# Masked cross-attention layer rewritten: strip scores, unnormalised weights, new queue order

## What is computed

```python
q = split_heads(layernorm(x) @ Wq + bq); k = split_heads(ctx @ Wk + bk); v = split_heads(ctx @ Wv + bv)
scores = einsum('bhqd,bhkd->bhqk', q, k) / sqrt(16)
scores = where(mask[:, None, :, :] > 0, -1e9, scores)
p = softmax(scores, axis=-1)
x = x + merge_heads(einsum('bhqk,bhkd->bhqd', p, v)) @ Wo + bo
```

## Time and profile before

| | us |
|---|---|
| median of 3 runs | 3196.28 (3191.54 to 3201.59) |
| the profiled execution | 3201.86 |
| its span, first to last instruction | 3200.1 |
| start of the program, weights, statistics | 0 to 34 |
| masked cross-attention | 34 to 1047 |
| state space layer | 1047 to 1586 |
| quantised network | 1586 to 1740 |
| sigmoid cross-attention (the other attention layer) | 1740 to 2436 |
| self-attention | 2436 to 2775 |
| experts | 2775 to 3200 |

### The profile page before, as it was taken

One profiled execution on the slowest core, in us unless ns is written; L12 is line 12 of the kernel. 1 busy time (PEld: TensorE's weight loads), 2 busy tenths in 40 slices (PEclk: granted clock), 3 DMA queues, 4 the chain that ended last, 5 costly groups with the idle time before them and its releaser, 6 DMA issues. The chain is left out here.

```text
span 3200.1 us, 85879 instructions
## 1 busy us (share of the span) xinstructions
PE 2706.9 (85%) x32700; PEld 2118.3 (66%) x32700; DVE 2312.3 (72%) x5209; ACT 1905.3 (60%) x4534; POOL 1931.9 (60%) x2135
## 2 busy tenths in 40 slices
PE   3999999999998489998677999999995788546998
PEld 2877777777777355555344788888884666434776
DVE  4999999999998387777634677777775788663443
ACT  2666767676666577767233677777773666343333
POOL 4888788888885477777300766666662677233332
PEclk9999999999999688988688999999997999757999
DMA  5121111111110000000000221111210000352110
GB/s 144 42 61 61 42 61 50 53 61 42 61 48 2 20 1 1 1 1 1 14 16 16 93 61 57 53 59 61 61 47 16 2 2 2 121 182 74 38 38 28
DMA packets 87375, 143.57 MB, mean 45 GB/s; under 512 B 10784, under 2 KB 74144, under 8 KB 80704
## 3 DMA queue, kind: packets, MB, share of 16 engines
q1 hardware_dynamic: 82304, 123.52, 12.4%
q0 software_dynamic: 4672, 14.57, 1.3%
HBM read 123.37 MB, written 14.69 MB: 43 GB/s over the span
## 5 line engine op out<-in xcount | busy, mean ns | idle before, releaser
L376 POOL TENSOR_SCALAR x_prob<-x_prob,x_rs 128x257 f32<-128x257 f32 x512 | 247.8, 484 | 173.1 <-DVE x_rs L852 141.6
L705 ACT ACTIVATE x_prob<-x_prob,x_nm 128x257 f32<-128x257 f32 x512 | 254.3, 498 | 152.6 <-DVE x_nm L846 152.5
L2119 DVE TENSOR_TENSOR_SCAN m_s<-m_a,m_psD 128x1024 f32<-128x1024 f32 x128 | 284.9, 2267 | 2.3 <-PE m_psD L1946 2.2
L1420 DVE SCALAR_TENSOR_TENSOR x_pTl<-x_psS,x_pTh 128x1024 f16<-128x1024 f32 x128 | 156.7, 1225 | 145.3 <-ACT x_pTh L1328 145.3
L843 DVE CUSTOM_DVE_ANT_0 x_prob<-x_psS,x_masked,x_prob 128x256 f32<-128x256 f32 x512 | 217.3, 481 | 4.5
L2058 ACT ACTIVATE m_a<-m_dt,m_rate 128x248 f32<-128x248 f32 x512 | 206.8, 492 | 0.0
L1108 POOL TENSOR_TENSOR x_qbdh<-x_qh,all_mask4h 128x1024 f16<-128x1024 f16 x32 | 60.6, 1895 | 217.5 <-DVE x_ql L1401 217.5
L1830 POOL TENSOR_TENSOR m_s<-m_s 128x1024 f32<-128x1024 f32 x64 | 150.5, 2352 | 67.8 <-DVE m_s L2119 67.8
L3003 ACT ACTIVATE e1t_g<-e1t_psH,e1t_bias 128x128 f32<-128x128 f32 x312 | 89.2, 368 | 171.0 <-PE e1t_psH L2952 171.0
L689 ACT ACTIVATE x_kh<-x_psK,x_bk 128x256 f16<-128x256 f32 x256 | 107.5, 471 | 118.6 <-PE x_psK L263 116.1
L861 DVE TENSOR_TENSOR x_pTl<-x_psT,x_pTh 128x512 f16<-128x512 f32 x256 | 164.2, 682 | 5.6 <-ACT x_pTh L676 3.0
(11 more groups left out here) (599 smaller groups left out, 11913.9 us busy)
## 6 DMA issues: line engine op xcount, KB each, us to landing
x_ctx<-in_ctxT SPq DMA_DIRECT2D x32, 1028.0 KB, 6.3
x_ctx<-in_ctxT SPq DMA_DIRECT2D x32, 1024.0 KB, 5.9
x_mraw<-in_mask SPq DMA_DIRECT2D x128, 128.5 KB, 2.8
e1r_stage<-in_L_ffn_w SPq DMA_DIRECT2D x16, 1024.0 KB, 5.0
e_rows<-e1r_pad POOLq DMA_DIRECT2D x1, 5070.0 KB, 19.6
e1t_row<-e_rows SPq DMA_DIRECT2D x39, 130.0 KB, 2.1
all_xres<-in_x SPq DMA_DIRECT2D x1, 4096.0 KB, 14.2
x_vxr<-x_vx SPq DMA_DIRECT2D x128, 32.0 KB, 3.4
```

The source lines that it names most:

```text
L376: last = pool.tensor_scalar(prob[n][:, h, :], prob[n][:, h, :], rs[n][:, h:h + 1], PS, ALU.mult, ALU.mult)
L705: last = act.activation(prob[n][:, h, :], prob[n][:, h, :], ACT.Exp, bias=nm[n][:, h:h + 1], scale=SC, accum_out=sm[n][:, h:h + 1])
L1420: dve.scalar_tensor_tensor(pT[c % 4][1][:].rearrange("p r k n -> p (r k n)"), psS[c % 2][:], PS, pT[c % 4][0][:].rearrange("p r k n -> p ( ...
L2119: dve.tensor_tensor_scan(states, rates, psD[at % 2][:], 0.0, ALU.mult, ALU.add).then_inc(scan_done, 1)
```

## The change

`masked_attention` takes the place of `cross_attention`. What it does:

- Scores use the twin layer's form: contraction over 64 partitions, two row strips at a time into two banks, 12 matmuls of 256 columns of which two can run side by side.
- One VectorE instruction for each strip scales the scores by -SC, adds the mask and takes the row's minimum, so that the result goes to the exponential as its bias directly. The exponentials wait strip by strip.
- The weights are not normalised. Their sums are spread over a diagonal by GpSimd (`spread_sums`), summed to the heads' rows on TensorE (`denominators`) once a group, and the extracted outputs are multiplied by the reciprocal of 256 columns (`normalise`).
- The last key's keys and values for all 128 batches are made once, ahead of the loop. Its values go through DRAM and come back broadcast to all partitions, 512 KB a group (`load_vx`); GpSimd multiplies them by the last weight (`value_last`), and four fp32 matmuls a batch add them.
- The mask is turned into numbers on GpSimd (`to_add`), not on VectorE. GpSimd also copies the last score into its column (`place_last`).
- More turns of buffers: keys and values 4, `prob` and `pT` 3.
- The queues are in a new order. A slot b, j = b % 4, g = b // 4, is run by every engine for b = 0 to 135.

The core of it:

```diff
+        @block.sync ...
+            def load(g):
+                wait(sync, ctx_split, (g - 1) * GB)
+                sync.dma_start(ctx32[g % 2][:], d["ctxT"][g][:, :, :, 0:LAST]).then_inc(ctx_in[g % 2], 16)
+            def load_mask(g):
+                wait(sync, mask_done, g)
+                src = d["mask"][g * GB:(g + 1) * GB].rearrange("j q k -> q j k")
+                for h in range(4):
+                    sync.dma_start(mraw[T * h:T * h + T], src).then_inc(mask_in, 16)
+            def load_vx(g):
+                wait(sync, pv_last, (g - 1) * GB)
+                src = vx_dram[g * GB:(g + 1) * GB, :].rearrange("(a j) n -> a j n", a=1).to_broadcast([P, GB, D])
+                sync.dma_start(vxr[g % 2][:], src).then_inc(vxr_in[g % 2], 16)
+            load(0); load_mask(0); load(1)
+            sync.wait_ge(vx_done, 1)
+            sync.dma_start(vx_dram, vx32[:]).then_inc(vx_out, 16)
+            sync.wait_ge(vx_out, 16)
+            for g in range(NT):
+                load_vx(g)
+                if g > 0:
+                    load_mask(g)
+                if g > 1:
+                    load(g)
+        @block.gpsimd ...
+            def split(b):
+                pool.wait_ge(ctx_in[g % 2], 16 * (g // 2 + 1))
+                wait(pool, v_mm, b - 7)
+                pool.tensor_scalar(hi[:, j], src, 1.0, 1.0, ALU.mult, ALU.mult).then_inc(ctx_hi, 1)
+                pool.wait_ge(ctx_hi, b + 1)
+                pool.tensor_tensor(lo[:, j], src, hi[:, j], ALU.subtract).then_inc(ctx_split, 1)
+            def to_add(g):
+                pool.wait_ge(mask_in, 64 * (g + 1))
+                wait(pool, s_min, 4 * GB * (g - 1))
+                wait(pool, last_done, g - 1)
+                pool.tensor_scalar(mlast[g % 2][:], mraw[:, :, LAST], 0.0, BIG * SC, ALU.is_gt, ALU.mult)
+                pool.tensor_scalar(masked[g % 2][:], mraw[:, :, 0:LAST], 0.0, -BIG, ALU.is_gt, ALU.mult).then_inc(mask_done, 1)
+            def place_last(b):
+                pool.wait_ge(last_done, b // GB + 1)
+                wait(pool, t_mm, b - NP + 1)
+                wait(pool, pv_last, b - NP + 1)
+                pool.tensor_copy(prob[b % NP][:, :, LAST], lastv[b // GB % 2][:, b % GB, :]).then_inc(placed, 1)
+            def value_last(b):
+                pool.wait_ge(exp_done, b + 1)
+                pool.wait_ge(vxr_in[g % 2], 16 * (g // 2 + 1))
+                wait(pool, pv_mm, b - 1)
+                pool.tensor_tensor(pv32[b % 2] (128x256), vxr[g % 2][:, j], prob[b % NP][:, :, LAST] broadcast, ALU.mult)\
+                    .then_inc(pv_last, 1)
+            def spread_sums(g):
+                pool.wait_ge(exp_done, (g + 1) * GB)
+                wait(pool, sum_mm, g)
+                pool.tensor_tensor(sums[:] (128x512), eye_q broadcast, sm[g % 2] broadcast, ALU.mult).then_inc(sums_done, 1)
+            for b in SLOTS:
+                batch(value_last, b - 1)
+                if j == 2: group(spread, g + 1)
+                batch(split, b + GB)
+                if j == 0: group(spread_sums, g - 1); group(to_add, g + 1)
+                if j == 1: group(add_bo, g)
+                batch(place_last, b + 1)
+        @block.tensor ...
+            def scores(b):
+                pe.wait_ge(k_lo, b + 1)
+                wait(pe, s_min, 4 * b)
+                for c in range(C):
+                    for q, k in ((0, 0), (0, 1), (1, 0)):
+                        for r in range(RG):
+                            rows = slice(64 * r, 64 * r + 64)
+                            pe.matmul(psS[:, r * 512 + c * LAST:...], qbd[g % 2][q][rows, c, j], K[b % NK][k][rows, c, :], ...)
+            for b in SLOTS:
+                batch(scores, b)
+                if j == 0: group(output, g - 2)
+                batch(keys, b + 2)
+                if j == 1: group(queries, g + 1)
+                if j == 2: group(denominators, g - 1)
+                if j == 3: group(last_scores, g + 1)
+                batch(turn, b - 1)
+                batch(values, b)
+                if j == 0: group(xnT, g + 1)
+                batch(attend, b - 2)
+        @block.scalar ...
+            for b in SLOTS:
+                if b % 2 == 0 and 0 <= b - 4 < NB: extract((b - 4) // 2)
+                batch(exps, b)            # waits s_min strip by strip
+                batch(hi_pT, b - 1)       # psT x PS -> pT hi, 1024 columns at once
+                if j == 1: group(hi_q, g + 1)
+                batch(hi_k, b + 2)
+                if j == 0: group(hi_xn, g + 1)
+                if j == 3: group(hi_ob, g - 1)
+                batch(hi_v, b)
+        @block.vector ...
+            def minima(b):
+                dve.wait_ge(placed, b + 1)
+                dve.wait_ge(s_mm, b + 1)
+                for s in range(4):
+                    dve.tensor_tensor_reduce(prob[b % NP][:, s, 0:LAST], psS[:, s * LAST:(s + 1) * LAST],
+                                             masked[g % 2][:, j, :], -SC, lastv[g % 2][:, j, s:s + 1], ALU.add, ALU.min,
+                                             nm[b % NP][:, s:s + 1]).then_inc(s_min, 1)
+            def normalise(g):
+                dve.wait_ge(sum_mm, g + 1)
+                dve.wait_ge(o_ext, 2 * g + 2)
+                dve.reciprocal(shares[:], psA).then_inc(share_done, 1)
+                dve.wait_ge(share_done, g + 1)
+                dve.tensor_tensor(row, row, shares[:], ALU.mult).then_inc(o_norm, 1)
+            for b in SLOTS:
+                batch(lo_v, b - 1)
+                batch(minima, b)
+                if b % 2 == 0 and 0 <= b - 4 < NB: extract((b - 4) // 2)
+                if j == 0: group(residual, g - 2)
+                if j == 2: group(normalise, g - 1)
+                if j == 3: group(last_values, g + 1)
+                batch(lo_pT, b - 1)
+                if j == 1: group(lo_q, g + 1); group(ln, g + 2)
+                batch(lo_k, b + 2)
+                if j == 0: group(lo_xn, g + 1)
+                if j == 3: group(lo_ob, g - 1)
```

More of the change, by code:

```diff
@@ L267, in both, with batch @@
-        def both(pair, f):
-            return (f(pair[0]), f(pair[1]))
-        LASTI = NT // 2 - 1
-        def run(eng, body):
-            for i in range(LASTI + 1):
-                body(i)
-        def preps(i, gp):
-            return not (isinstance(i, int) and i == LASTI and gp == 1)
-        def started(i, c, lag):
-            return not (isinstance(i, int) and 8 * i + c - lag < 0)
+        SLOTS = range(NB + 2 * GB)
+        def batch(f, b):
+            if 0 <= b < NB:
+                f(b)
@@ new lines, in _ @@
+            for t in kxp:
+                pool.memset(t[:], 0.0).then_inc(kx_zeroed, 1)
+            pool.wait_ge(const_in, 112)
+            for b in range(2):
+                split(b)
+            to_add(0)
+            spread(0)
+            for b in range(2, GB):
+                split(b)
+            place_last(0)
+            for b in SLOTS:
+                g, j = b // GB, b % GB
+                batch(value_last, b - 1)
+                if j == 2:
+                    group(spread, g + 1)
+                batch(split, b + GB)
+                if j == 0:
+                    group(spread_sums, g - 1)
+                    group(to_add, g + 1)
+                if j == 1:
+                    group(add_bo, g)
+                batch(place_last, b + 1)
@@ new lines, in attend @@
+                for c in range(C):
+                    to = (c * 2 + b % 2) * P
+                    for r in range(RG):
+                        last = pe.matmul(psO[64 * r:64 * r + 64, to:to + P],
+                                         pv32[b % 2][:, c * P + 64 * r:c * P + 64 * r + 64], con["ident"][:],
+                                         start=False, stop=True, skip_group_check=True)
+                last.then_inc(pv_mm, 1)
+            last_keys()
+            xnT(0)
+            keys(0)
@@ new lines, in lo_pT, with lo_k @@
+            def lo_pT(b):
+                dve.wait_ge(pt_hi, b + 1)
+                wait(dve, pv_mm, b - NW + 1)
+                dve.scalar_tensor_tensor(flat(pT[b % NW][1]), psT[:], PS, flat(pT[b % NW][0]), ALU.mult, ALU.subtract)\
+                    .then_inc(pt_lo, 1)
+            def lo_k(b):
+                dve.wait_ge(k_hi, b + 1)
+                wait(dve, s_mm, b - NK + 1)
+                for h in range(C):
+                    last = dve.scalar_tensor_tensor(K[b % NK][1][:, h, :], psK[:, h * LAST:(h + 1) * LAST], bk[:, h:h + 1],
+                                                    K[b % NK][0][:, h, :], ALU.add, ALU.subtract)
@@ L959, in _ @@
[L959 to L973 removed]
+            dve.wait_ge(const_in, 112)
+            for t in (bq, bk, bv):
+                dve.tensor_scalar(t[:], t[:], WS, None, ALU.mult).then_inc(bias_ready, 1)
@@ new lines, in _ @@
+            last.then_inc(kx_lo, 1)
+            lo_xn(0)
+            ln(1)
+            lo_k(0)
+            lo_q(0)
+            lo_k(1)
+            last_values(0)
+            for b in SLOTS:
```

(20 more changed lines are left out.)

879 lines of the change are left out of this document (286 added, 593 removed).

## The result

| | before | after |
|---|---|---|
| median, us | 3195.06 (4 runs) | 3447.55 (3441.18 to 3454.10, 4 runs) |
| ratio, 95% interval | | 1.0788 (1.0760 to 1.0816) |
| profiled execution, its span | 3201.86, 3200.1 | 3441.18, 3439.3 |
| first and last row minimum | 59.1, 1029.5 | 58.5, 1272.8 |

The kernel is 7.9% slower, in the place and by the mechanism of the forecast, and 62 us beyond its 3385. That is 8 us above the main case's own range (3340 to 3440) but inside that of the clock's case (3415 to 3475) and inside the overall range, 3190 to 3470. All of the loss lies in the rewritten layer: its row minima now span 1214.3 us where they spanned 970.4, 243.9 more, while the rest of the program is 4.7 us shorter.

A forecast was written before the change was run, and what follows sets the result against it. VectorE's queue was taken as the bound. From 3202 us, a shorter circuit (-89), a stall in 30 groups (+280) and edges (-3) gave 3390, less 6 for the median: 3384, said as 3385; overall range 3190 to 3470.

The forecast's parts named there:

- main case: Masked layer: late context load plus GpSimd's slow mask conversion stall VectorE once a group; 3385 us, chance 0.45.
- clock's case: TensorE idles some 10 us per stall, then runs partly at 1.2 GHz, late in slots 1 and 2: 3415 to 3475, chance 0.08.
- The stall: VectorE before minima(4g-3): a 22.55 us chain where two slots need 13.2; 9.3 us a group, +280 us in all.
- the start: From minima(4g-5) until value_last(4g-5) can start on GpSimd, held by attend(4g-7): 4.6 us.
- The transfer: SP's queue: GpSimd's split waits for the group's context, requested behind the vx load and masks; taken as 9.3 us.
- D: Time of the context's transfer behind the vx load and mask DMAs: 9.2 to 11.2 us, 9.3 taken.
- M: Time of to_add, the mask's conversion, on GpSimd: 4.3 us taken, with 1.2 or 0.9 as the cheap end.
- The circuit: VectorE and ScalarE, lo_pT(b-1) behind the next batch's exponentials: 27.7 us a group against 30.5, -89 us.
- The edges: Layer's start 1 to 4 us later, its end about 4 shorter, dropped constants about 1: -3 us together.
- The one that was faster: Loads are covered, chain from minima(4g-5) ends within 13.2 us, nothing stalls: 3104 us, chance 0.17.
- The cheap mask pass: to_add on GpSimd takes 1.2 or 0.9 us, so the stall is 3.1 to 3.4 less a group: 3290, chance 0.24.
- GpSimd's work in slots 1 to 3: After the stall GpSimd catches up, with under 5 us of work a slot against 7.

The follow-up runs named there:

- the fastest version: Changed kernel with loads first, mask's pass on VectorE, reciprocal before the spread, and pv32 with three buffers: 3066.66 us, ratio 0.9599 to the kernel before.
- the version with three cuts: Changed kernel with the context first behind the same wait, the mask's pass on VectorE and three pv32 buffers: 3109.63 us, ratio 0.9725 to the kernel before.
- four kernels that stall: Changed kernel (3447.6 us), and it with one edit each: context first behind the same wait (3341.3), mask's pass on VectorE (3324.5), pv32 with three buffers (3363.3).

## Why the prediction was right, and by how much each step was off

- **The stall.** Forecast 22.55 us from `minima(4g-5)` to `minima(4g-3)`, measured 23.53 (818.87 to 842.40), as the sum of slots 3 and 0 a median of 23.63. By its terms: the start 4.6, measured 824.25 - 818.87 = 5.38. TensorE's `keys` began at -0.37, not -0.6, `last_scores` took 0.64, not 0.4, attend's end to the product's start another 0.25 that I hadn't counted. The transfer 9.3, measured 10.43 (824.90 to 835.33). SP issued the five DMAs in 2.29 us, and the context was then 8.1 us under way, not 6.8, with the vx load and the masks in front of it. In front of them it is 6.4 us under way, so the bytes did queue in part, and of my two ends for D the 11.2 was the nearer. `spread_sums` 1.2, measured 1.07. M 4.3, measured 3.63: nearer the dear end, chosen by the row nearest in operation and not in shape. VectorE's idle time in the stall is 10.15 where 9.3 was forecast.
- **The circuit.** 6.5, 7.0, 7.55 and 6.7 for slots 0 to 3; without a stall 6.49, 7.34, 7.48 and 6.80. The one miss of note is `ln` at 0.75 instead of 0.40 in slot 1, which the forecast kept for the range. 28.1 us a group against 27.7, and the layer's minima 890.5 us long (59.1 to 949.6) where they were 970.4: the rewrite is worth 80 us where 89 were forecast.
- **Slot 2 in the stalled kernel**, 8.12 us at the median and 8.23 on average instead of 7.55: 0.68 in 32 groups, 22 us. The reciprocal itself took the forecast's time (1.76), but waited 0.69 for TensorE.

```profile
852.74 1.76 DVE L699 RECIPROCAL x_shares<-x_psM 128x256 f32<-128x256 f32 x1 [0.69 <-PE x_psM L430]
```

- **The clock.** I gave it 0.08 as a rival and it is a part of the result. In the stall TensorE is busy for 5.25 of 10 us, and after it the granted clock is 0.68 on average for 16 us, a mixture of 2.4 and 1.2 GHz; the rows are the windows of both, then us 842 to 858 of the fastest version, which has no stall:

```profile
832.00:842.00 10.00, 5.25 (x75) 4.56 (x73) 0.25 (x1) 0.00 (x0) 6.52 (x5) 1.00 0.16 51
842.00:858.00 16.00, 10.51 (x102) 7.24 (x102) 12.96 (x35) 9.37 (x28) 11.22 (x16) 0.68 0.01 1
```

```profile
842.00:858.00 16.00, 15.77 (x238) 13.17 (x237) 13.43 (x37) 11.57 (x34) 9.04 (x15) 1.00 0.11 34
```

The low clock stands in slots 1 and 2. Slot 1 hides it: its granted clock is 0.50 to 0.57 in the 30 groups that stall, and it is 6.91 us long, where the version with three cuts takes 6.96 at a clock of 1.00. Slot 2 doesn't: its mean is 8.31 us in these groups, 0.82 above the 7.49 of the version with the loads first and the mask on VectorE, 25 us in all. No run isolates the clock, but the trace nearly does. Over these 30 groups the length of slot 2 goes with its granted clock at a correlation of -0.99 (worked out from the minima's starts and the clock's records), and TensorE is busy for all of it in these two groups, one of the longest and the shortest:

```profile
225.77:234.70 8.93, 8.93 (x82) 6.34 (x80) 7.38 (x18) 4.32 (x12) 4.89 (x7) 0.69 0.01 2
...
1082.29:1089.93 7.65, 7.65 (x84) 5.46 (x82) 7.27 (x18) 4.32 (x12) 5.12 (x7) 0.85 0.01 2
```

All four kernels that stall have the longer slot 2 (8.07 to 8.34), and none that doesn't except the one with TensorE's order changed. So the forecast's two cases, the dear pass and the clock, came true together. The clock's was priced at 1 to 3 us a group and cost 0.8.
- **The sum.** The layer's minima were forecast to last 27.7 x 31.75 + 280 = 1159.5 us and lasted 1214.3, 54.8 more: (23.70 - 22.55) x 30 = 34 from the chain by its mean, 22 from slot 2, slot 1 gives 4 back, and 2 or 3 are rounding in the forecast's terms. The edges gave -4.7 where -3 were put, though the first minima came at 58.5 and not 1 to 4 us later than 59.1. So the profiled execution lies 51 us above the forecast's 3390. The other 11 of the 62 are no part of the mechanism: I took 5 off for the median, as in the kernel before, and here the median lies 6 above the profiled execution.
- **The rivals.** The one that was faster needed a chain 6.4 us shorter than the forecast's. The run with three cuts took 3.5 + 4.1 + 2.8 = 10.4 off a chain of 23.5, which leaves 13.1, and is where it said: faster, with VectorE's wait for `place_last` all but gone. The cheap mask pass was wrong: 3.63 us, not 1.2. Wrong too, without a cost, was GpSimd's work in slots 1 to 3 as under 5 us each: in slot 2 `spread` alone is 1.99 + 1.89, and the slot's work some 6.4.

The Trainium skill (GPSIMD Engine Reference, section 4.1, Engine selection) calls a one-input pass on GpSimd roughly line-rate. The measurement here decides against it for this form: 3.63 us for 1024 columns, with a comparison, on int32, where the same pass took VectorE 0.68 us. The Trainium skill (SBUF — State Buffer, section on the two separate sides) has GpSimd exclude on a shared port VectorE's two-port forms, and its instructions with two SBUF inputs if GpSimd's reads SBUF. The traces agree: `ln` took 0.75 beside GpSimd's product and 0.41 without it. The normalising product took 1.02 on average when it started inside GpSimd's subtraction and 0.42 when it didn't; with one operand from PSUM it took 0.42 inside a GpSimd product too.

## What to carry to other kernels

List, for each DMA queue, what stands behind each wait, and add up the chain from that wait to the engine that sets the pace. A load whose own buffer is free loses its whole lead if it is issued behind a wait for another buffer, and the order of three calls was worth 9.5% of the changed kernel's time. When such a chain is a sum with a threshold, any few cuts that bring it below the threshold do as well as the cure, and none of them alone does.

When the stall is gone look at both queues that are next, not at the busier one: breaking VectorE's circuit took 0.25 us off an undisturbed group, since VectorE then waited as long for TensorE's scores as it had for `hi_pT`. And let a broadcast come after the expensive function, not before: 16 reciprocals instead of 256 were worth 41 us.

## What the runs showed of the hardware

- Strips on different rows of TensorE run side by side even with two matmuls of the same rows between them in the queue: twelve 64-row matmuls of 256 columns take 0.66 us in either order.
- 0.66 us more of matmuls a batch cost 0.18 us a batch, in a kernel whose TensorE is busy for 91% of the time.
- A pass with `is_gt` and `mult` from int32 costs 3.63 us for 1024 columns on GpSimd, 3.5 ns a column, against 1.2 ns a column for the mult-mult cast (0.62 for 512) and 0.66 ns on VectorE.
- VectorE's reciprocal costs by the column, 1.76 us for 256 from PSUM and 0.24 for 16.
- Behind a stall of 10 us in which TensorE was busy for half the time, its granted clock was 1.2 GHz for a part of the next 16 us; in the versions without a stall it was 1.00 over us 500 to 900, with TensorE busy for 91 to 97% of them. The exception is the one with TensorE's order changed: 0.98, at 93% busy, with single stretches at 1.2 GHz. Its busy share isn't the reason, since others lie on both sides of it.
- A VectorE instruction that GpSimd holds up ends a little after GpSimd's: `ln` 0.15 us after it, the normalising product with both operands in SBUF 0.28.
- A load of 1 MB, asked for 2.29 us after five others were begun on the same queue, was under way 8.2 us, and 6.4 when it was asked for before them.
